# A transformer layer on one core: the constant rows of the score stacks written by ScalarE, and the first loads waited for and sent in another way

## The reference

```python
qk = x @ W_attn + b_attn                      # 256 -> 512: queries and keys
y  = causal_attn(q, k, v=x)                   # softmax(q k^T / 4) v, per head
e  = v[:, :, 1:, :] - y[:, :, :-1, :]
k2 = x[:, :-1] @ W_k2 + b_k2
y2 = causal_attn(q[:, :, 1:, :], k2, e)       # a second attention on the error
x  = layernorm(x + proj(y) + proj(shift(y2)))
x  = layernorm(x + experts(x))                # experts on the routed tokens
```

## Time and profile before

| | us |
|---|---|
| median of 3 runs (lowest, highest) | 2521.51 (2519.04, 2525.44) |
| the profiled execution, time | 2529.61 |
| its span in the trace | 2527.9 |

### The profile page before, as it was taken

The page is one execution under the profiler, slowest core; times in us unless marked ns, Lnnn a source line. Parts: engine busy times, 40 slices in busy tenths (PEclk is TensorE's granted clock), DMA queues, the critical chain, the costliest instruction groups (busy, mean ns, idle before and its releaser), DMA issues.

```text
span 2527.9 us, 64943 instructions
## 1 busy us (share of the span) xinstructions
PE 2387.1 (94%) x19670; PEld 1307.0 (52%) x19670; DVE 2128.2 (84%) x9273; ACT 1759.7 (70%) x3388; POOL 1509.2 (60%) x2342
## 2 busy tenths in 40 slices
PE   2999999999999999999999999999999999999996
PEld 1555555555555555555555555555555555555454
DVE  2889888888898888888988888889888888898655
ACT  0377777777777767777777777777777777777652
POOL 2356666666666656666666666666666666665432
PEclk8699999999999999999999999999999999999998
DMA  5555565565555656555555565555555655455111
GB/s 94 95 92 96 87 108 108 107 118 106 101 100 98 105 103 112 107 100 102 101 97 112 106 117 107 99 99 102 101 109 106 120 107 99 99 101 93 54 62 47
DMA packets 187781, 251.22 MB, mean 99 GB/s; under 512 B 26768, under 2 KB 103192, under 8 KB 187416
## 3 DMA queue, kind: packets, MB, share of 16 engines
q1 hardware_dynamic: 187440, 247.07, 52.8%
HBM read 74.60 MB, written 16.78 MB: 36 GB/s over the span
## 4 chain that ended last, share of the span: by engine, by line
PE 67%; ACT 11%; POOL 8%; issue 8%; DVE 4%; SPq 1%; DMA 1%; ACTq 0%; POOLq 0%; DVEq 0%
PE out_t L612 20%; PE score_t L651 17%; PE misc L703 11%; PE score L662 7%; PE misc L744 5%; ACT heads_t L536 4%; ACT prob L518 4%; PE out_t L677 4%; POOL prob L429 3%; DVE junk L860 2%; POOL part_l L451 2%; PE score L803 1%; PE misc L730 1%; ACT part_f L528 1%; POOL y_sum L476 1%
## 5 line engine op out<-in xcount | busy, mean ns | idle before, releaser
L860 DVE CUSTOM_DVE_ANT_0 junk<-score,mask_rows 128x384 bf16<-128x384 f32 (+3 forms) x3584 | 1688.2, 515 | 275.5 <-PE score L662 241.5
L518 ACT ACTIVATE prob<-score_t 128x512 f32<-128x512 f32 x2560 | 1369.6, 600 | 456.2 <-PE score_t L651 455.3
L429 POOL TENSOR_SCALAR_AFFINE_SELECT prob<-prob 128x512 f32<-128x512 f32 (+1 forms) x1280 | 715.0, 562 | 831.9 <-ACT prob L518 831.5
L651 PE MATMUL score_t<-stack_q,stack_k 50*128 50x128 f32 (+5 forms) x4096 | 997.2, 360 | 21.4 <-DVE max_cols L860 2.4
L662 PE MATMUL score<-stack_k,stack_q 48*128 48x512 f32 (+3 forms) x4096 | 989.2, 348 | 12.4 <-DMA stack_q<-part_l 10.7
L651 PEld LDWEIGHTS score_t<-stack_q,stack_k 50*128 50x128 f32 (+1 forms) x4096 | 611.1, 186 | 572.9 <-ACT prob L518 295.0
L612 PE MATMUL out_t<-prob,value 128*17 128x512 f32 (+3 forms) x8192 | 673.4, 439 | 5.7 <-POOL prob L429 5.5
L662 PEld LDWEIGHTS score<-stack_k,stack_q 48*128 48x128 f32 x4096 | 616.3, 188 | 33.8 <-DVE max_cols L860 12.4
L860 DVE DVE_READ_ACCUMULATOR2_ANT max_cols<- 128x1 f32 x4096 | 339.4, 83 | 0.0
L612 PEld LDWEIGHTS out_t<-prob,value 128*17 128x17 f32 x8192 | 188.3, 97 | 283.0 <-issue 217.8
L451 POOL TENSOR_TENSOR part_l<-part_f,part_h 128x512 fp32r<-128x512 f32 x192 | 255.0, 1328 | 16.2
(11 more groups left out here) (98 smaller groups left out, 1718.4 us busy)
## 6 DMA issues: line engine op xcount, KB each, us to landing
stack_k<-part_h SPq DMA_DIRECT2D x512, 128.0 KB, 5.0
stack_k<-part_l SPq DMA_DIRECT2D x256, 128.0 KB, 4.6
stack_q<-part_h SPq DMA_DIRECT2D x256, 128.0 KB, 4.2
x_full<-x_turned SPq DMA_DIRECT2D x32, 512.0 KB, 10.4
x_in<-L_attn_x SPq DMA_DIRECT2D x32, 512.0 KB, 14.5
stack_q<-part_l SPq DMA_DIRECT2D x128, 128.0 KB, 5.1
resid<-L_attn_x SPq DMA_DIRECT2D x32, 512.0 KB, 5.6
layer_out<-resid SPq DMA_DIRECT2D x31, 512.0 KB, 6.1
```

The lines of the kernel that those rows point to most:

```text
L429: e.affine_select(out=view, in_=view, compare_op=ALU.is_ge, fill=0.0, base=-unit_parts(unit)[1], pattern=[[0, runs], [0, cut], [1, P]], ch ...
L518: e.activation(prob[pair % RING][:, slot % 2 * 512:slot % 2 * 512 + 512], score_t[time % KEY_DEPTH][:, :], ACT.Exp, scale=1.0 / np.sqrt(HE ...
L651: done = e.matmul(score_t[now % KEY_DEPTH][:, col:col + n], keys[rows, pair, kb * P:(kb + 1) * P], stack_q[b % 2][rows, pair, kb * P:token ...
L860: e.tensor_tensor_reduce(junk[count % JUNK][:, 0:n], score[number % MAX_DEPTH][:, col:col + n], mask, 1.0, -3e38, ALU.add, ALU.max, max_co ...
```

## The change

The tile `ones` and the 12 transfers from it are gone. POOL makes the identity matrix right after its first memset. DVE makes from it two small tiles `row_ones`, a column each of 128 ones and zeros (four instructions of 1 or 2 columns), and ACT writes each of the four key stacks whole, 128 partitions by 4096 elements, as 0 times the identity plus that column (`fill_stack`): the stacks of batch 0 before its first other work, those of batch 1 behind the transfers of the first and the second query piece. `s_weights` becomes `s_wq` (queries' and keys' weights and `bias_qk`), `s_wk2` and `s_wproj`. DVE splits `wq` as soon as `s_wq` is full, and `wk2` after the first piece has left PE; PE's first piece waits for the split of `wq` alone, and for each half of `x_t` apart. The transfers of batch 0's two query pieces are issued by ACT instead of SP. Every piece, in all batches, is sent in two steps: four transfers of the high part behind the cast, two of the low part behind the subtraction. `x_in`, `wp` and `bias2` are loaded behind piece 2, and batch 1's `x_full` behind them; `bias2` is doubled where DVE first copies `x_in` to the values.

```diff
-        ones = nc.alloc_sbuf_tensor_at("ones", [2 * MAX_PARTS, pairs, tokens], F32R, offset=prob_at)
-        wq_full = nc.alloc_sbuf_tensor_at("wq_full", [P, halves, 2 * halves, P], F32, offset=prob_at + 4 * pairs * tokens)
-        wk2_full = nc.alloc_sbuf_tensor_at("wk2_full", [P, halves, halves, P], F32, offset=prob_at + 5 * pairs * tokens)
+        wq_full = nc.alloc_sbuf_tensor_at("wq_full", [P, halves, 2 * halves, P], F32, offset=prob_at)
+        wk2_full = nc.alloc_sbuf_tensor_at("wk2_full", [P, halves, halves, P], F32, offset=prob_at + pairs * tokens)
+
+        row_ones = [nc.alloc_sbuf_tensor_at(f"row_ones{a}", [P, 3], F32, offset=prob_at + 2 * pairs * tokens + 32 * a) for a in range(2)]
...
+        def fill_stack(e, a, i):
+
+            stack = (stack_k, stack_k2)[a][i]
+            zeros = bass.AP(ident[:, :].tensor, ident[:, :].offset, [list(ident[:, :].ap[0]), [0, pairs], [0, tokens]])
+            e.activation(stack[:, :, :], zeros, ACT.Identity, bias=row_ones[a][:, 2:3], scale=0.0).then_inc(s_filled[2 * a + i], 1)
...
+        def stack_piece(e, kind, hf, b, n):
+
+            stack = {"q": stack_q, "k": stack_k, "k2": stack_k2}[kind][b % 2]
+            terms = PARTS_Q if kind == "q" else PARTS_K
+            if b < 2 and kind != "q":
+                e.wait_ge(s_filled[(2 if kind == "k2" else 0) + b], 1)
+            if b >= 2:
+                reader = UNITS * (b - 2) + (0 if kind == "k" else GROUPS) + (hf + 1) * GROUPS // halves - 1
+                e.wait_ge(s_key, SLOTS * (reader + 1))
+            for part, tile in enumerate((part_h[n % 2], part_l[n % 2])):
+                e.wait_ge(s_split, 2 * n + part + 1)
+                for term in range(TERMS):
+                    if terms[term] == part:
+                        for side in range(SIDES):
+                            row = SIDE * side + term * HEAD_DIM
+                            e.dma_start(stack[row:row + HEAD_DIM, hf * pairs_half:(hf + 1) * pairs_half, :].bitcast(F32),
+                                        tile[SIDE * side:SIDE * (side + 1), :].bitcast(F32)).then_inc(s_stack[kind, hf], 16)
...
-            e.dma_start(wq_full[:, :, :, :], w_attn.rearrange("(h p) (w n) -> p h w n", p=P, n=P)).then_inc(s_weights, 16)
-            e.dma_start(bias_qk[:, :], b_qk).then_inc(s_weights, 16)
-            e.dma_start(wk2_full[:, :, :, :], w_k2.rearrange("(h p) (w n) -> p h w n", p=P, n=P)).then_inc(s_weights, 16)
-
-            R, M = SCORE_ROWS, MAX_PARTS
-            e.wait_ge(s_ones, 2)
-            for side in range(SIDES):
-                for i in range(2):
-                    e.dma_start(stack_k[i][SIDE * side + R:SIDE * side + R + M, :, :].bitcast(F32), ones[0:M, :, :].bitcast(F32)).then_inc(s_rows, 16)
-                    e.dma_start(stack_k2[i][SIDE * side + R + M:SIDE * side + R + 2 * M, :, :].bitcast(F32), ones[0:M, :, :].bitcast(F32)).then_inc(s_rows, 16)
-                    e.dma_start(stack_k2[i][SIDE * side + R:SIDE * side + R + M, :, :].bitcast(F32), ones[M:2 * M, :, :].bitcast(F32)).then_inc(s_rows, 16)
-            e.dma_start(x_in[:, :, :], x[0].rearrange("(t p) c -> p t c", p=P)).then_inc(s_x, 16)
-            e.dma_start(wp[:, :, :], w_proj.rearrange("(h p) n -> p h n", p=P)).then_inc(s_weights, 16)
-            e.dma_start(bias2[:, :], b_proj.rearrange("(o n) -> o n", o=1).to_broadcast([P, width])).then_inc(s_weights, 16)
+            e.dma_start(wq_full[:, :, :, :], w_attn.rearrange("(h p) (w n) -> p h w n", p=P, n=P)).then_inc(s_wq, 16)
+            e.dma_start(bias_qk[:, :], b_qk).then_inc(s_wq, 16)
+            e.dma_start(wk2_full[:, :, :, :], w_k2.rearrange("(h p) (w n) -> p h w n", p=P, n=P)).then_inc(s_wk2, 16)
...
-                if (place, slot) == (0, 8) and 1 <= b < batches:
+                if (place, slot) == (3 if b == 1 else 0, 8) and 1 <= b < batches:
...
+                if piece and not (piece[0] == "q" and piece[2] == 0):
+                    stack_piece(e, *piece)
+                    if piece[3] == N_PIECES // 3:
+                        e.dma_start(x_in[:, :, :], x[0].rearrange("(t p) c -> p t c", p=P)).then_inc(s_x, 16)
+                        e.dma_start(wp[:, :, :], w_proj.rearrange("(h p) n -> p h n", p=P)).then_inc(s_wproj, 16)
+                        e.dma_start(bias2[:, :], b_proj.rearrange("(o n) -> o n", o=1).to_broadcast([P, width])).then_inc(s_wproj, 16)
...
             e.memset(ident[:, :], 1.0).then_inc(s_const, 1)
+            e.wait_ge(s_const, 1)
+            e.affine_select(out=ident[:, :], in_=ident[:, :], compare_op=ALU.is_equal, fill=0.0,
+                            base=0, pattern=[[1, P]], channel_multiplier=-1).then_inc(s_const, 1)
             e.memset(x_next[:, :, :], 0.0).then_inc(s_const, 1)
...
+            e.wait_ge(s_ones, 4)
+            fill_stack(e, 0, 0)
+            fill_stack(e, 1, 0)
...
+                if piece and piece[0] == "q" and piece[2] == 0:
+                    stack_piece(e, *piece)
+                    fill_stack(e, piece[1], 1)
...
-                                e.wait_ge(s_weights, WEIGHTS)
+                                e.wait_ge(s_wsplit, 2)
+                            if kind == "k2" and b == 0:
                                 e.wait_ge(s_wsplit, 4)
-                            if n % N_PIECES == 0:
-                                e.wait_ge(s_xsplit, 2 * halves * (b + 1))
...
+                        if n % N_PIECES == 0:
+                            e.wait_ge(s_xsplit, 2 * (halves * b + c + 1))
...
-            e.memset(ones[0:2 * MAX_PARTS, :, :].bitcast(F32), 0.0).then_inc(s_ones, 1)
-            e.wait_ge(s_ones, 1)
-            e.memset(ones[0:MAX_PARTS, :, :].bitcast(F32), 1.0).then_inc(s_ones, 1)
-            e.memset(out_t[:, :], 0.0).then_inc(s_ones, 1)
+            e.wait_ge(s_const, 2)
+            for a in range(2):
+                first = SCORE_ROWS + MAX_PARTS * a
+                e.tensor_tensor(row_ones[a][:, 0:2], ident[:, first:first + 2], ident[:, SIDE + first:SIDE + first + 2],
+                                ALU.add).then_inc(s_ones, 1)
+                e.wait_ge(s_ones, 2 * a + 1)
+                e.tensor_tensor(row_ones[a][:, 2:3], row_ones[a][:, 0:1], row_ones[a][:, 1:2], ALU.add).then_inc(s_ones, 1)
+            e.memset(out_t[:, :], 0.0).then_inc(s_empty, 1)
+            for i, (parts, full) in enumerate(((wq, wq_full), (wk2, wk2_full))):
+                if i == 0:
+                    e.wait_ge(s_wq, 32)
+                else:
+                    e.wait_ge(s_wk2, 16)
+                    e.wait_ge(s_piece, 1)
+                e.tensor_copy(parts[HIGH][:, :, :, :], full[:, :, :, :]).then_inc(s_wsplit, 1)
+                e.wait_ge(s_wsplit, 2 * i + 1)
+                e.tensor_tensor(parts[LOW][:, :, :, :], full[:, :, :, :], parts[HIGH][:, :, :, :].bitcast(F32),
+                                ALU.subtract).then_inc(s_wsplit, 1)
...
+                    if b == 0:
+                        e.wait_ge(s_wproj, 32)
+                        e.tensor_tensor(bias2[:, :], bias2[:, :], bias2[:, :], ALU.add).then_inc(s_bias, 1)
```

More of the change, by code:

```diff
@@ L146, in build_layer @@
         misc = ps("misc", 512)
-        s_weights, s_rows, s_next, s_resid, s_out = (sem(f"s_{n}") for n in ("weights", "rows", "next", "resid", "out"))
+        s_wq, s_wk2, s_wproj, s_next, s_resid, s_out = (sem(f"s_{n}") for n in ("wq", "wk2", "wproj", "next", "resid", "out"))
         s_x, s_xt = sem("s_x"), sem("s_xt")
@@ L152, in build_layer @@
         s_maxrow = [sem(f"s_maxrow{i}") for i in range(2)]
-        s_const, s_ones, s_bias, s_wsplit = (sem(f"s_{n}") for n in ("const", "ones", "bias", "wsplit"))
+        s_const, s_empty, s_ones, s_bias, s_wsplit = (sem(f"s_{n}") for n in ("const", "empty", "ones", "bias", "wsplit"))
+        s_filled = [sem(f"s_filled{i}") for i in range(4)]
         s_key, s_qry, s_pv, s_turned, s_piece, s_yt_pe, s_proj, s_neg_pe = (
@@ L408, in _ @@
                 e.memset(tile[:, :], 0.0).then_inc(s_const, 1)
[L409 to L411 removed]
+            e.wait_ge(s_const, 8)
             for a in range(2):
```

38 lines of the change are left out of this document (10 added, 28 removed).

## The result

| | us |
|---|---|
| before: median of 4 runs (lowest, highest) | 2520.28 (2519.03, 2525.44) |
| after: median of 4 runs (lowest, highest) | 2489.89 (2488.96, 2490.87) |
| ratio, with its 95% interval | 0.9882 (0.9861 to 0.9902) |
| profiled execution: before, after | 2529.61, 2490.87 |
| its span: before, after | 2527.9, 2488.8 |

The change makes the kernel 30.4 us faster, 1.2%; the prediction was 27.9. The two spans differ by 39.1, because the profiled execution of before was itself some 9 us above its median. The changed kernel was timed again beside two of the sets of experiments, where its median was 2495.73 and 2493.60, against 2521.17 and 2521.18 of before: 25.4 and 27.6 us. All 13 runs of it together have their median at 2491.57, the 23 runs of before compared with them at 2521.17: 29.6 us. Two slow runs of before, of 3382 and 11532 us, are left out of all comparisons.

The account below looks back on a forecast made before the run. PE, busy for 94% of the span, was taken as the bound, so only an earlier start could pay: 2529.6 less 27.9 gives 2501.7, and timed runs 8.1 us lower give a median of 2493.6 us; range 2483 to 2505.

Parts of the forecast that it names:

- The forecast case: Opening: first score 27.9 us earlier with nothing lost behind it, median 2493.6 us; chance 0.56.
- Part 1: PE's first matmul: starts at 8.3 us, its second half at 9.85, moving piece 0 by 25.3 us.
- neither the semaphore nor the transfers were worth anything alone: PE's start: weights' own semaphore and removed transfers pay only together, since either alone leaves the other holding PE.
- Part 2: Two ACT fills ahead of piece 0: 3.7 us each, from 2.5 to 9.9 us, hidden with 1.4 us to spare.
- The end of 6.8 us: Slow estimate per ACT fill: two would end at 16.1 us and hold piece 0 for 4.8 us.
- Part 3: Pieces 0 and 1 into the stacks: first issue at 12.75 us, both landed 15.3 us later, at 28.0.
- Part 4: Third fill, pieces 2 and 3: chain ends at 27.5 us, landing at 28.0 sets first score; no wait at 43.4.
- The rival in which the loads take the queries' place: Piece 3's queries land last, at 46.7 us against 43.4: 3.3 us back, 2496.9 us; chance 0.10.
- The rising clock: PE after the first score: 2.4 GHz level saves up to 9.0 us more, 2484.6 us; chance 0.12.
- The slower rival: 186 later pieces: early high parts cost PE 0.15 us each, cancelling the gain, or 0.3 for 2549 us; chance 0.06.
- Later batches: Behind the opening: four transfers of a piece leave 1.3 us earlier from the same queue, gaining nothing.

Follow-up runs that it names:

- before_fills: Kernel before with ACT fills replacing the 12 transfers of ones, one semaphore kept for all weights: median 2501.12 us, ratio 0.9926.
- before_semaphores: Kernel before with separate semaphores for wk2 and for wp and bias2, the 12 transfers of ones kept: median 2502.18 us, ratio 0.9936.
- queries_by_sp: Changed kernel with batch 0's query pieces issued by SP again, fills in place on ACT: median 2495.95 us, ratio 0.9899.
- late_fills: Changed kernel with both fills of batch 1's key stacks moved behind the second query piece: median 2495.09 us, ratio 0.9896.
- after_third: The changed kernel itself timed again, beside a repeat with one-step sending from batch 1 on: 2493.60 us, ratio 0.9885.
- one_step_later: Changed kernel with pieces from batch 1 on sent behind both parts, as before: median 2492.14 us, ratio 0.9900; repeated at 2495.46 us, ratio 0.9897.
- one_fill_first: Changed kernel with one ACT fill ahead of piece 0 and three behind the second query piece: one run, 2498.18 us.

## Why the prediction was right, and where it was not

**The mechanism and the total.** The forecast case, an opening moved as a block with nothing lost behind it, is what happened. The time is 3.7 us below the forecast of 2493.6; the opening is 1.8 us short of its 27.9 at the first score and 3.1 short at the first exponential, and some 5 us came from elsewhere (30.4 less 24.8; 0.6 and 2.8 us in the two later sets). Two errors of opposite sign made the total look better than the working, and that is luck.

**Part 1: the mis-sized term.** `s_wq` full at 6.3 us is right (DVE starts at 6.38). The 0.70 and 1.22 us of DVE came from a stretch of before in which POOL was idle. Beside POOL they take 0.92 and 2.17, and POOL's split of `x_t` ends at 11.3 us instead of 9.8. The step that failed is to let both splits run side by side at their times alone. The two engines took turns: from POOL's first cast, which ends at 6.75, the durations alone of DVE's cast, POOL's subtraction and DVE's subtraction, 0.70, 1.26 and 1.22, less 0.14 each, give 9.5 us, and there DVE's split ended. So PE starts at 9.75 where 8.3 was forecast, its second half at 11.37 where 9.85 was, and what follows is later still: bias addition 13.05 for 11.35, first stack transfer 14.84 for 12.75, since POOL's cast of piece 0 takes 0.95 us for 0.61 beside DVE's split of `wk2`. In before_fills, where the two hardly meet, the same instructions take 1.22 and 0.61 us again. The sentence that neither the semaphore nor the transfers were worth anything alone is wrong: 16.7 and 17.7 us were measured. It looked at what releases PE before and took the other wait to be as late, without working out its time. In before_semaphores SP sends the transfers while PE already works; in before_fills the loads of `wp` and `bias2` come sooner by themselves, and DVE starts at 9.47 where it started at 30.44.

**Part 2: right.** Fills of 3.7 us, estimated from shapes of 4 and 512 elements, measured 3.69 to 3.71, and hidden. The end of 6.8 us, from the form with a scale read from a tile, did not apply.

**Part 3: right in its length.** 15.3 us from the first issue to the landing of the first queries, measured 15.0 in the changed kernel and 15.0 to 15.05 in three variants. The issues on ACT took 0.7 us each on average for 0.6, of no consequence, as queries_by_sp shows. SP's longest issue in the opening is 1.29 us, and not 1.25; nothing rests on it.

**Part 4: right by a smaller margin than it had.** The landing was to end last by 0.5 us before the third fill's chain. Both ended at 29.8: PE was through with piece 3, and its weight load then waited 0.82 us for the queries. late_fills and queries_by_sp show that the landing alone would have held the score there. At 43.4 us no wait was forecast for unit 2; with everything 1.8 us late that is 45.2, and the score came at 46.12, its queries having taken 11.69 us to land. **The rival in which the loads take the queries' place** was therefore there in small, 0.9 us for its 3.3: in queries_by_sp, with one load behind the queries, the score came at 45.24. The copy of the values came at 49.12, where 73.94 - 27.9 = 46.0 had been set down: 3.0 us behind unit 2's first score for 2.7 before, so it is late for the same reason.

**The rising clock** did not come. The matmuls are 0.43 us apart up to 80 us, 3 us later than the 77 of the forecast, and late_fills reads 0.50 over 30 to 80 us with PE busy for 46.26 of 50. In a third profile of the changed kernel (after_third) the level was 2.4 GHz twice for 3.4 us, at 21 and 45 us, and 1.2 from there to 79. That PE now ran straight from piece 3 into the scores changed nothing. The Trainium skill, "TensorE: Matmul & The Clock Gate", Part 1, says that the gate opens after sustained activity; a stretch with PE busy for 46.26 of 50 us at the low level disagrees, as the earlier trace rows did.

**The slower rival**, early high parts that cost PE time in every piece, is refuted by the total and by the pair around one_step_later: with the early parts the kernel is no slower, and a batch takes 72.07 us with them and without (one_step_later).

**Later batches: "nothing" holds for a batch as it usually goes, and not for the total.** A batch takes 72.10 us in the profile of before and 72.07 in that of the changed kernel (medians from one addition of the residual to the next), which makes 1 us in 30 batches. So the two steps speed no batch, and what was gained behind the opening came in single batches. The profiles show two things there. The first is the clock: the execution of before had three short drops ahead of 2300 us, of 3.4 us each (windows, columns as above):

```profile
128.00:138.00 10.00, 8.96 (x74) 4.35 (x72) 7.67 (x37) 5.93 (x12) 3.70 (x7) 0.83 0.57 85
...
156.00:166.00 10.00, 9.28 (x70) 4.70 (x71) 7.52 (x36) 6.65 (x13) 6.64 (x11) 0.83 0.40 82
...
928.00:932.00 4.00, 4.00 (x21) 2.06 (x22) 2.70 (x12) 2.31 (x5) 1.47 (x3) 0.57 1.09 143
```

Over the first two the distance between the two profiles grows from 25.0 to 27.8 us, and the changed kernel's profile has none ahead of 2300 us. But the profile of one_step_later had two such drops, at 108 and 136 us, so they belong to an execution as much as to a kernel. The second is POOL's wait for the residual's load, 9.4 against 2.2 us. In before the batch that ends with the wait of 2.3 us at 921 us is 2.4 us longer than the usual, and the next one, with a wait of 2.4 us and the third drop, 3.8 us. Shifting the batches against the transfers changes how often the load is late. Which of these makes the 0.6 to 5.6 us between the opening's 24.8 and the gains of the three sets is not settled: each varies from run to run by as much as is to be explained (the variants' profiles have 0 to 5.6 us of such waits).

## What to carry to other kernels

When a change puts two engines' work side by side, the durations from a trace in which each worked alone are lower bounds. Here, for VectorE and GpSimd splitting 32-bit tiles in SBUF, the right sum was one engine's instructions and the other's, one after the other. In an opening that fills buffers by DMA, count from the first issue to the last landing: who issued, and how soon the last issue came, was worth nothing for the first score here while the DMA engines had work. An instruction on an engine that is only 60% busy can still be in the wrong slot, if PE waits for what is queued behind it: moving one addition of 2.4 us four slots was worth 17 us in the kernel before.

## What the runs showed of the hardware that was not expected

**DVE and POOL take turns.** On tiles in SBUF, casting and subtracting 32-bit data: DVE's subtraction of 128x1024 took 1.22 us alone and 1.51 to 2.17 beside POOL, its cast 0.70 alone and 0.92 to 1.08; POOL's subtraction of 128x512 1.26 alone and 1.58 to 2.13, its cast 0.61 alone and 0.95 to 1.60. ACT's fill beside them made no difference (one_fill_first). In each of these meetings an instruction ended its time alone, less 0.13 to 0.15 us, behind the other engine's last one. Even the smallest waited: DVE's three one-column instructions, 0.55 us alone, took 1.73 us in the changed kernel and ended at 16.12, with POOL's subtraction (timeline):

```profile
14.39 1.73 DVE L871 SCALAR_TENSOR_TENSOR sum_floor<-ident,sum_floor 128x1 f32<-128x1 f32 x3
...
14.83 1.28 POOL L459 TENSOR_TENSOR part_l<-part_f,part_h 128x512 fp32r<-128x512 f32 x1
```

Before the change DVE's memset (6.08 to 9.55 us) lay beside POOL's subtraction at 8.54 without lengthening it, and in the changed kernel DVE's maxima from PSUM (0.69 us each from 31.29) lie beside POOL's subtraction at 31.21, which takes 1.27. So it is not any work of DVE.

**The clock differs between executions of almost the same instructions.** Pieces 1 to 3 of the opening ran at the 1.2 GHz level in the changed kernel (0.43 us from matmul to matmul) and at the 2.4 GHz level in late_fills and one_fill_first (0.23), all three with piece 0 at the lower. In these two it fell back during the last matmuls of piece 3, at 23 us, before the scores.
